# Attention with latent keys on one core: weight transposes moved from TensorE to DMA, and weight products moved to another row block

## The reference

```python
q = (x @ wq).reshape(b, s, H, QH).transpose(0, 2, 1, 3)
kva = x @ wkv_a
ckv, k_pe = (kva[..., :LORA], kva[..., LORA:])
ckv = ckv * jax.lax.rsqrt(jnp.mean(ckv * ckv, axis=-1, keepdims=True) + EPS) * kv_norm_scale
kv = (ckv @ wkv_b).reshape(b, s, H, NOPE + VD).transpose(0, 2, 1, 3)
scores = jnp.einsum('bhqd,bhkd->bhqk', qs, ks_) * scale
attn = jax.nn.softmax(jnp.where(causal, scores, min), axis=-1)
out = jnp.einsum('bhqk,bhkd->bhqd', attn, v).transpose(0, 2, 1, 3).reshape(b, s, H * VD) @ wo
x = x + out + (jnp.einsum('btd,rde->bte', xn, factors) / math.sqrt(rank) + bias)
```

## Time and profile before

| | us |
|---|---|
| median of 3 runs | 1497.72 (1497.66 to 1498.66) |
| profiled execution, span from first to last instruction | 1496.9 |
| TensorE busy in it | 1469.3 |
| VectorE, ScalarE, GpSimd busy | 1014.5, 965.7, 911.3 |

### The profile page before, as it was taken

One profiled execution on the slowest core, in us unless ns is written; L12 is line 12 of the kernel. 1 busy time (PEld: TensorE's weight loads), 2 busy tenths in 40 slices (PEclk: granted clock), 3 DMA queues, 4 the chain that ended last, 5 costly groups with the idle time before them and its releaser, 6 DMA issues.

```text
span 1496.9 us, 25751 instructions
## 1 busy us (share of the span) xinstructions
PE 1469.3 (98%) x7908; PEld 755.5 (50%) x7908; DVE 1014.5 (68%) x2563; ACT 965.7 (65%) x2404; POOL 911.3 (61%) x919
## 2 busy tenths in 40 slices
PE   6999999999999999999999999999999999999998
PEld 5544555555555545445444444445545555555554
DVE  7877677877777766656556565556666666676777
ACT  7877767677876567566566666665546665654554
POOL 3688777776665456575465656566645655664553
PEclk9999999999999999999999999999999999999999
DMA  6599999988777597787577677886856677754564
GB/s 202 152 199 203 211 193 186 191 163 158 157 157 132 127 193 149 140 178 139 118 145 141 137 133 145 173 151 130 162 112 136 137 139 152 156 141 95 115 132 110
DMA packets 646615, 227.84 MB, mean 152 GB/s; under 512 B 599376, under 2 KB 612176, under 8 KB 646096
## 3 DMA queue, kind: packets, MB, share of 16 engines
q1 hardware_dynamic: 646480, 226.20, 74.2%
HBM read 65.67 MB, written 17.83 MB: 56 GB/s over the span
## 4 chain that ended last, share of the span: by engine, by line
PE 92%; POOL 2%; DVE 2%; ACT 2%; DMA 1%; issue 1%; SPq 0%; POOLq 0%; DVEq 0%; ACTq 0%
PE ps L426 18%; PE ps L428 18%; PE ps L427 18%; PE ps L577 7%; PE ps L582 7%; PE ps L583 7%; PE ps L578 7%; PE ps L579 7%; POOL st L1408 2%; ACT ex L812 1%; DMA acc<-x_in 0%; DVE stats L944 0%; PE ps L450 0%; DVE acc L1227 0%; DMA pT<-st 0%
## 5 line engine op out<-in xcount | busy, mean ns | idle before, releaser
L1408 POOL TENSOR_TENSOR st<-ex,st 128x512 f16<-128x512 f32 (+3 forms) x640 | 637.8, 1015 | 488.9 <-ACT st L822 478.8
L812 ACT ACTIVATE ex<-ps,nm,scales 128x512 f32<-128x512 f32 (+3 forms) x640 | 452.0, 709 | 456.3 <-DVE nm L1193 439.8
L1174 DVE TENSOR_REDUCE gm<-ps 128x1 f32<-128x512 f32 (+1 forms) x384 | 249.0, 669 | 170.0 <-PE ps L583 166.0
L822 ACT ACTIVATE st<-ex 128x512 f16<-128x512 f32 (+3 forms) x640 | 343.0, 562 | 6.1 <-ACT ex L812 0.4
L577 PE MATMUL ps<-kTh,q 128*128 128x512 f16 (+3 forms) x640 | 222.3, 347 | 4.5 <-ACT ex L812 2.1
L426 PE MATMUL ps<-pT,vH 128*128 128x512 f16 (+3 forms) x640 | 222.1, 347 | 2.9 <-DMA pT<-st 2.9
L582 PE MATMUL ps<-kRh,q 128*128 128x512 f16 (+3 forms) x640 | 222.2, 347 | 0.0
L583 PE MATMUL ps<-kRl,q 128*128 128x512 f16 (+3 forms) x640 | 222.1, 347 | 0.0
L579 PE MATMUL ps<-kTh,q 128*128 128x512 f16 (+3 forms) x640 | 222.1, 347 | 0.0
L578 PE MATMUL ps<-kTl,q 128*128 128x512 f16 (+3 forms) x640 | 222.1, 347 | 0.0
L427 PE MATMUL ps<-pT,vH 128*128 128x512 f16 (+3 forms) x640 | 222.1, 347 | 0.0
(11 more groups left out here) (202 smaller groups left out, 2144.3 us busy)
## 6 DMA issues: line engine op xcount, KB each, us to landing
wA<-w_abs SPq DMA_DIRECT2D x48, 256.0 KB, 2.9
wV<-w_vo SPq DMA_DIRECT2D x48, 256.0 KB, 2.9
pT<-st SPq DMA_TRANSPOSE x640, 3.2
fland<-factors_in SPq DMA_DIRECT2D x28, 256.0 KB, 3.1
wP<-w_pe SPq DMA_DIRECT2D x24, 256.0 KB, 3.0
wsq<-wq_in SPq DMA_DIRECT2D x16, 256.0 KB, 3.8
wso<-wo_in SPq DMA_DIRECT2D x16, 256.0 KB, 3.0
w_abs<-wA SPq DMA_DIRECT2D x16, 256.0 KB, 2.2
```

Of the source, the lines that this page charges most:

```text
L812: e.activation(ex[:, n % NEX, 0:keys], s_bank(n)[:, 0:keys], ACT.Exp, bias=nm[:, (i * QT + r) % 4:(i * QT + r) % 4 + 1], scale=scales[:, p ...
L822: e.activation(stage(n, keys)[:, :, 0, :], ex[:, n % NEX, 0:keys].rearrange("p (t n) -> p t n", n=P), ACT.Copy).then_inc(z["a_pH"], 1)
L1174: e.tensor_reduce(m, b, AX_X, ALU.max).then_inc(z["v_max"], 1)
L1408: e.tensor_tensor(s[:, :, 1, :], ex[:, n % NEX, 0:keys].rearrange("p (t n) -> p t n", n=P), s[:, :, 0, :], ALU.subtract).then_inc(z["g_pL" ...
```

## The change

The weights are no longer transposed on TensorE. VectorE splits them in SBUF, still in the layout in which they were loaded, from `wsq`, `wsk`, `wsv` into the new `wtq` and `wtk` (L1037 and L1056, L1051 and L1063 of the changed kernel), and SyncE issues two DMA transposes a head: `turn_wq` of 8 float16 blocks of 128 x 128 into `wX`, `turn_kv` of 2 or 4 into `wKV`. The split of head 1 moves into the prologue, that of head 2 to row block 1 of unit 0, and that of later heads i + 2 to row block 1 of unit i. `w_abs` and `w_vo` on TensorE wait for the landing of the transposes; from unit 1 on they move from the end of row block 2 to row block 3, behind the output product and ahead of the rest. The work of TensorE has one group fewer in the rotation of the three banks for "tq" and one for "tkv".

```diff
-        out += [[("tq", 1), ("tkv", 1), ("sq1", 2)], [("wabs", 1), ("nrm", 2), ("wpe", 2)],
-                [("tq", 2), ("tkv", 2), ("q", 1), ("wpe_low", 2)], [("wabs", 2)]][r]
+        out += [[("sq1", 2)], [("wabs", 1), ("nrm", 2), ("wpe", 2), ("tq", 2), ("tkv", 2)],
+                [("q", 1), ("wpe_low", 2)], [("wabs", 2)]][r]
...
+    if r == 3 and i and i + 2 < H:
+        out.append(("wabs", i + 2))
+    if r == 3 and 1 <= i <= H:
+        out.append(("wvo", i - 1))
     if r == 0:
-        if i % 2 and i + 2 < H:
-            out.append(("tq", i + 2))
...
     if r == 1:
         if i and i % 2 == 0 and i + 2 < H:
-            out += [("wpe", i + 2), ("tq", i + 2)]
+            out.append(("wpe", i + 2))
+        if i and i + 2 < H:
+            out.append(("tq", i + 2))
...
     if r == 2:
-        if 1 <= i <= H:
-            out.append(("wvo", i - 1))
-        if i and i + 2 < H:
-            out.append(("wabs", i + 2))
...
-IN_BANKS = ("q", "pe", "tkv", "wvo", "tq", "wabs", "out", "ffn")
+IN_BANKS = ("q", "pe", "wvo", "wabs", "out", "ffn")
...
-                e.wait_ge(z["v_tq"], h + 1)
-                e.wait_ge(z["v_tkv"], h + 1)
+                e.wait_ge(z["d_tq"], 16 * (h + 1))
+                e.wait_ge(z["d_tkv"], 16 * (h + 1))
...
+            def wq_high(h):
+
+                e.wait_ge(z[f"d_wq{h % 2}"], 16 * (h // 2 + 1))
+                e.wait_ge(z["v_w2"], h // 2 + 1)
                 if h:
-                    e.wait_ge(z["p_wabs"], h)
+                    e.wait_ge(z["d_tq"], 16 * h)
+                e.tensor_scalar(wtq[:, :, 0, :], wsq[:, h % 2, :, :], scales[:, h // 2, 0:1], None, ALU.mult).then_inc(
+                    z["v_tq_hi"], 1)
...
+            def wq_low(h):
                 e.wait_ge(z["v_tq_hi"], h + 1)
+                e.scalar_tensor_tensor(out=wtq[:, :, 1, :], in0=wsq[:, h % 2, :, :], scalar=scales[:, h // 2, 0:1],
+                                       in1=wtq[:, :, 0, :], op0=ALU.mult, op1=ALU.subtract).then_inc(z["v_tq"], 1)
...
+            def turn_wq(h):
+
+                e.wait_ge(z["v_tq"], h + 1)
+                if h:
+                    e.wait_ge(z["p_wabs"], h)
+                e.dma_start_transpose(wX[:, :, :, :].rearrange("p k a n -> p (k a) n"),
+                                      wtq[:, :, :, :].rearrange("p k a n -> p (k a n)")).then_inc(z["d_tq"], 16)
+
+            def turn_kv(m):
+
+                e.wait_ge(z["v_tkv"], m + 1)
+                if m:
+                    e.wait_ge(z["p_wabs"], min(m, H))
+                if m > 3:
+                    e.wait_ge(z["p_wvo"], m - 3)
...
             store_chunk(0)
+            turn_wq(0)
+            turn_kv(0)
             load_wq(2)
...
             store_pe(0)
+            turn_wq(1)
+            turn_kv(1)
             load_wq(3)
...
+                    if r == (1 if i else 2):
+                        if i + 2 < H:
+                            turn_wq(i + 2)
+                        if i + 2 <= H + 2:
+                            turn_kv(i + 2)
                     if i < NU:
                         for p in range(chunk(i) + 1):
                             transpose(i, r, p)
```

More of the change, by code:

```diff
@@ L256, in build @@
         wa = sb("wa", [P, 2, KE, QH], F16)
-        wX = sb("wX", [P, 2, E], F16)
-        wKV = sb("wKV", [P, 2, 2 * P], F16)
+        wX = sb("wX", [P, KE, 2, P], F16)
+        wKV = sb("wKV", [P, 2, 2, P], F16)
+        wtq = sb("wtq", [P, KE, 2, P], F16)
+        wtk = sb("wtk", [P, 2, 2, P], F16)
         wsq = sb("wsq", [P, 2, KE, P], F32)
@@ L478, in w_abs @@
                 b = free_bank(("wabs", h))
-                e.wait_ge(z["v_tq"], h + 1)
-                e.wait_ge(z["v_tkv"], h + 1)
+                e.wait_ge(z["d_tq"], 16 * (h + 1))
+                e.wait_ge(z["d_tkv"], 16 * (h + 1))
                 for k4 in range(KE):
                     cols = slice(k4 * P, (k4 + 1) * P)
-                    ins = three(b[:, cols], [wX[:, a, cols] for a in range(2)], [wKV[:, a, 0:P] for a in range(2)])
+                    ins = three(b[:, cols], [wX[:, k4, a, :] for a in range(2)], [wKV[:, 0, a, :] for a in range(2)])
                 ins.then_inc(z["p_wabs"], 1)
@@ L488, in w_vo @@
                 e.wait_ge(z["v_wo"], h + 1)
-                e.wait_ge(z["v_tkv"], h + 4)
-                three(b, [wKV[:, a, P:2 * P] for a in range(2)], [wV[:, h % 2, a, :] for a in range(2)]).then_inc(
+                e.wait_ge(z["d_tkv"], 16 * (h + 4))
+                three(b, [wKV[:, 1, a, :] for a in range(2)], [wV[:, h % 2, a, :] for a in range(2)]).then_inc(
                     z["p_wvo"], 1)
@@ L1058, in kv_transpose @@
-            def kv_transpose(m):
-                b = bank(("tkv", m))
-                parts = []
-                if m < H:
-                    e.wait_ge(z["v_w2"], m // 2 + 1)
-                    parts.append((slice(0, P), scales[:, m // 2, 1:2]))
-                if m >= 3:
-                    e.wait_ge(z["v_vw"], m - 2)
-                    parts.append((slice(P, 2 * P), vsc[:, m - 3, 0:1]))
-                e.wait_ge(z["p_tkv"], m + 1)
-                if m:
-                    e.wait_ge(z["p_wabs"], min(m, H))
-                if m > 3:
-                    e.wait_ge(z["p_wvo"], m - 3)
-                for cols, size in parts:
-                    ins = e.tensor_scalar(wKV[:, 0, cols], b[:, cols], size, None, ALU.mult)
-                ins.then_inc(z["v_tkv_hi"], 1)
+                    e.wait_ge(z["d_tq"], 16 * h)
@@ new lines, in wq_high, with kv_high @@
+                e.tensor_scalar(wtq[:, :, 0, :], wsq[:, h % 2, :, :], scales[:, h // 2, 0:1], None, ALU.mult).then_inc(
+                    z["v_tq_hi"], 1)
+            def kv_high(m):
+                if m < H:
+                    e.wait_ge(z["g_sk"], m // 2 + 1)
+                    e.wait_ge(z["v_w2"], m // 2 + 1)
+                if m >= 3:
+                    e.wait_ge(z["g_sv"], m - 2)
+                    e.wait_ge(z["v_vw"], m - 2)
+                if m:
+                    e.wait_ge(z["d_tkv"], 16 * m)
+                for part, w, size in kv_parts(m):
+                    ins = e.tensor_scalar(wtk[:, part, 0, :], w, size, None, ALU.mult)
+                ins.then_inc(z["v_tkv_hi"], 1)
@@ L1076, in kv_transpose, with kv_low @@
+            def wq_low(h):
+                e.wait_ge(z["v_tq_hi"], h + 1)
+                e.scalar_tensor_tensor(out=wtq[:, :, 1, :], in0=wsq[:, h % 2, :, :], scalar=scales[:, h // 2, 0:1],
+                                       in1=wtq[:, :, 0, :], op0=ALU.mult, op1=ALU.subtract).then_inc(z["v_tq"], 1)
+            def kv_low(m):
                 e.wait_ge(z["v_tkv_hi"], m + 1)
-                for cols, size in parts:
-                    ins = e.scalar_tensor_tensor(out=wKV[:, 1, cols], in0=b[:, cols], scalar=size,
-                                                 in1=wKV[:, 0, cols], op0=ALU.mult, op1=ALU.subtract)
+                for part, w, size in kv_parts(m):
+                    ins = e.scalar_tensor_tensor(out=wtk[:, part, 1, :], in0=w, scalar=size, in1=wtk[:, part, 0, :],
+                                                 op0=ALU.mult, op1=ALU.subtract)
@@ L1495, in load_wv @@
                 if m > 4:
[L1496 removed]
+                    e.wait_ge(z["v_tkv"], m - 1)
                     e.wait_ge(z["a_sqv"], m - 4)
```

79 lines of the change are left out of this document (33 added, 46 removed).

## The result

The changed kernel took 1502.44 us in the median of 13 executions (1499.93 to 1504.83), the kernel before 1497.97 us (1497.11 to 1498.66): ratio 1.0028, 95% interval 1.0021 to 1.0035. It is 4.5 us slower, where 1496.0 us and a gain of 1.7 us were forecast. The profiled execution is the shortest of the 13: 1499.93 us, span 1498.1. So two things are to be explained: the loss in the execution shown here, and the 2.5 us more of the median one. The two profiled spans differ by 1.2 us only, but that understates the first.

The account below looks back on a forecast made before the run. TensorE, busy 98% of the span, was taken as the bound. Span 1496.9 - 8.9 + 4.9 - 2.2 + 0.5 + 1.0 + 2.0 + 1.0 = 1495.2 us, so 1496.0 us measured; range 1490.5 to 1501.5.

Parts of the forecast that it names:

- SyncE's queue: Two more issues a unit, 2.56 us, make SyncE late in early units, about level with TensorE: +1.0 us, bounds 0 and 9.
- What is removed: Weight transposes leave TensorE: 10.5 us in all, 8.9 us of it behind 78 us, where TensorE is the bound.
- The first wait: Unit 0, head 2's product: TensorE waits for DMA-turned weights from 78.2 to 83.1, 4.9 us, bounds 4.0 and 7.0.
- VectorE, "nothing on the path": Row block 1: splitting from SBUF costs 0.5 to 0.9 us more a head, covered by VectorE's idle time: no cost.
- The prologue: Before unit 0: head 0's split, two issues and a landing delay TensorE's product by +0.5 us, bounds -0.5 and 2.
- The rival on the slow side: SyncE's queue sets the pace of units 1 to 7, values waiting for pT in every unit: 1504 us, chance 0.15.
- What that gives back: From 70 to 140 us: SyncE keeps issuing, so waits for pT and exponentials go: -2.2 us, bounds 0 and 2.2.
- The gaps: Even units 4 to 10, row block 1: TensorE returns earlier and waits 0.5 us for a bank: +2.0 us, bounds 0 and 3.
- the positional bank: Even units: the positional product waits 0.2 us for a PSUM bank VectorE frees: +1.0 us over five units, bounds 0 and 2.

Follow-up runs that it names:

- GpSimd out of the way: Changed kernel with unit 0's four bias additions on GpSimd placed two each in row blocks 2 and 3, not one per row block: 1502.23 us.
- the kernel with the products behind the values: Changed kernel with the weight products of units 1 to 16 moved behind the value products in row block 3: 1511.64 us, ratio 1.0092.
- the three versions from head 4 on: Changed kernel with heads 0 to 3 turned by TensorE: 1495.43 us; also early loads: 1494.13 us; also products back in row block 2: 1498.36 us.
- the two with stops: Kernel before with six TensorE stops put into units 20 to 30, waiting on a 512-byte transfer: 1590.18 us; on a 4-byte one: 1527.21 us.
- the better one: Changed kernel with heads 0 to 3 turned by TensorE, their buffers' loads waiting for its transposes, not VectorE's split: 1494.13 us, ratio 0.9973.

## Why the prediction was wrong

The forecast put the change at -1.7 us; it came out at +4.5. The step that failed is the one on SyncE's queue, which was taken for a tie. SyncE came to head 3's own pair 8.1 us after its split had ended, TensorE stopped for 2.70 us and then ran at half clock. Unit 1, which by the terms of the forecast was to be about 2 us shorter, was 2.5 us longer. The rest is 3 us of the median execution in the prologue. By term:

- **What is removed**: right. In odd units the whole 0.66 us is gained (32.36 to 31.70 in unit 3).
- **The first wait**: right in size and wrong in what showed, so partly luck. Unit 0 grew by 4.68 us; the plain wait, 4.76 us, is seen only with GpSimd out of the way. In the changed kernel it is 2.92 us for exponentials, 0.29 us for wKV and 1.6 us of clock.
- **VectorE, "nothing on the path"**: this step failed. I priced the split from the mean of a form from SBUF, 0.5 to 0.9 us more a head, without asking what made that mean: its eight operations took 0.74 to 1.52 us. It took 4.5 us in unit 0 where it takes 1.9 us by itself, and in the prologue query 0 came 1.3 us later (a wait of 1.89 us at 55.73, 0.6 before), because GpSimd was at work. It cost little only because SyncE was later still.
- **The prologue, +0.5 us, bounds to 2**: mis-sized. 1.25 us at the start of unit 0 in the profiled execution, most of it query 0, and some 3 us more in the median one: the 1 MB store that the forecast named and did not price. Behind it each issue of head 0's pair took 2.14 us in place of 1.28.
- **SyncE's queue, "a tie", +1.0 us**: the step that failed hardest. I checked the margin of the pT transposes and not that of head 3's own pair. Its split ended at 102.0; SyncE came to it at 110.1:

```profile
103.06 5.39 SPq L1591 DMA_TRANSPOSE pT<-st  x4
...
110.11 1.24 SPq L1600 DMA_TRANSPOSE wX<-wtq  x1
111.45 2.28 SPq L1610 DMA_TRANSPOSE wKV<-wtk  x1
```

  TensorE, at the product at 113.2, waited 2.70 us. The rival on the slow side named this queue and a unit-by-unit pace; what came was one stop in unit 1, and no wait for pT in units 2 to 7. That the time lies near that rival's is luck.
- **What that gives back, -2.2 us**: nearly right. The 1.06 us wait for pT went, and of 1.1 us of short waits for exponentials 0.4 us stayed. Unit 2 was another 1.5 us shorter than before, which the forecast did not have.
- **The clock**: in no term, a cost left out without a reason. It was 1.6 and 1.7 us in the profiled execution, more than all by which that execution (+2.3 us at unit 17) is slower than the kernel before.
- **The gaps, +2.0, and the positional bank, +1.0**: right in mechanism. 0.28 us in row block 2 (the rest of the gap between 7.94 and 8.22), where 0.5 us was forecast, and 0.22 us in row block 3 of each even unit, where 0.2 us was: 2.5 us in units 2 to 10.

The cost lay where the kernel starts, and the gain where it runs.

## What to carry to other kernels

Before work is moved to a queue, take the moment at which each moved item can start and the moment at which the queue comes to it, item by item, from the first one on; a queue that keeps pace in the body may have no room in the first two units, and the cure is to begin the new scheme after them. Expect 1.7 us of half clock on top of a stop of TensorE, as behind 16 of the 20 stops of 2.5 to 4.8 us in these profiles, and look how much of a saving the next bound downstream gives back before counting it. Price a VectorE operation that moves from PSUM to SBUF by what GpSimd does at that moment, not by its mean.

## What the runs showed of the hardware

- After a stop TensorE often ran at the lower clock, 1.2 GHz: for 3.4 us after 2.70 and 2.92 us of standing still in the changed kernel, for 6 and 8 products of 512 columns after 3.70 and 4.15 us, not after 3.21 us, and for 6 to 11 products after stops of 11 to 13 us. The same stop in the prologue had it in one kernel and not in another, and two stops of 0.87 and 1.06 us close together had it as well. In the kernel with the products behind the values 14 products were slow behind a stop of 2.93 us.
- VectorE operations of 0.28 to 0.35 us (128x128, from SBUF) took 1.14 to 1.3 us while GpSimd worked. From PSUM the operation of 0.35 us took 0.34 to 0.35 us in all of its 32 executions.
- The two DMA transposes right behind a 1 MB store took 2.14 us each to issue. The median of such a transpose in the same kernel was 1.24 us (8 blocks) and 1.20 us (2 or 4), with single ones of 2.28 and 2.33 us far from that store.
- From the issue of a transfer of 512 bytes in 128 pieces (718.02) to the product that waited for it (728.53) it took 10.5 us, for one of 4 bytes (717.57 to 718.85) 1.3 us.
- All but one of the executions of the three versions from head 4 on last 2.4 to 3.1 us longer than their spans, those of the other kernels 1.8 to 1.9 us, but for the two with stops (1.7 to 2.8 us). So of the 5.1 us that the better one gains in the median span only 4.1 us arrive in the median time. Why stays open.
